# A context-attention stage: the outermost loop of TensorE's program written out for its fourteen middle chunks

## The reference, cut to what matters

```
q      = layernorm(x) @ Wq                  (32 tokens)
k, v   = split(ctx @ Wkv)                   (257 keys of 256 features)
k, v   = with null_kv as one more key and value
sim    = q . k / sqrt(64)                   (16 heads x 32 x 258)
out    = softmax(sim) @ v, heads joined
x      = x + layernorm(out @ Wout) * ln_scale + ln_bias
```

## Time and profile before

| what | value |
|---|---|
| median of three runs | 4516.92 us |
| the profiled execution's own time | 4519.83 us |
| its span (first to last instruction) | 4518.0 us |
| mean granted TensorE clock over the span | 0.917 of full speed |
| TensorE matmul busy | 3780.1 us, 84% of the span |
| VectorE, ScalarE, GpSimd busy | 63%, 44%, 18% of the span |
| the stage's score matmuls begin and end | 96.5 us to 1511.5 us |

### The profile page before, as it was taken

One profiled execution on the slowest core, in us unless ns is written; L12 is line 12 of the kernel. 1 busy time (PEld: TensorE's weight loads), 2 busy tenths in 40 slices (PEclk: granted clock), 3 DMA queues, 4 the chain that ended last, 5 costly groups with the idle time before them and its releaser, 6 DMA issues. The chain is left out here.

```text
span 4518.0 us, 116638 instructions
## 1 busy us (share of the span) xinstructions
PE 3780.1 (84%) x46470; PEld 2881.3 (64%) x46470; DVE 2838.7 (63%) x5431; ACT 1998.1 (44%) x4327; POOL 818.4 (18%) x797
## 2 busy tenths in 40 slices
PE   5999999999999873279998679889997777879776
PEld 4888888888888642257666356656664345656454
DVE  2766666666666587442223776567776956878683
ACT  2332333233223364533333333478887745654323
POOL 0000000000000041200000036555553012200160
PEclk7999999999999986689999889989998989989878
DMA  4655555555555145310000023222220000000000
GB/s 127 133 120 119 120 119 120 120 120 120 119 119 123 39 125 183 123 70 1 0 0 21 5 101 145 79 71 67 72 71 27 0 6 3 0 13 1 9 3 24
DMA packets 307757, 320.58 MB, mean 71 GB/s; under 512 B 43440, under 2 KB 295249, under 8 KB 299873
## 3 DMA queue, kind: packets, MB, share of 16 engines
q1 hardware_dynamic: 307296, 313.84, 27.3%
HBM read 286.44 MB, written 27.05 MB: 69 GB/s over the span
## 5 line engine op out<-in xcount | busy, mean ns | idle before, releaser
L3891 PE MATMUL c_psA<-c_kc,c_qt 128*128 128x257 f32 x2048 | 497.6, 398 | 78.0 <-issue 77.4
L3912 PEld LDWEIGHTS c_psB<-c_pt,c_vc 32*128 32x128 f32 x16384 | 471.8, 188 | 44.5 <-issue 44.5
L3912 PE MATMUL c_psB<-c_pt,c_vc 32*128 32x128 f32 x16384 | 496.2, 274 | 1.9 <-DVE c_vo L4091 1.9
L3891 PEld LDWEIGHTS c_psA<-c_kc,c_qt 128*128 128x128 f32 x2048 | 399.9, 201 | 139.5 <-issue 81.3
L4015 ACT ACTIVATE c_sc<-c_psA,c_mx 128x257 f32<-128x257 f32 x512 | 215.4, 473 | 534.4 <-DVE c_mx L4102 534.4
L637 PEld LDWEIGHTS f_psY<-f_w_down,f_hT 128*128 128x128 f32 x2560 | 302.7, 192 | 64.7 <-issue 48.4
L680 ACT ACTIVATE f_hT<-f_psH,f_b_up 128x512 f32<-128x512 f32 x320 | 214.3, 688 | 281.1 <-PE f_psH L627 276.5
L4098 DVE TENSOR_REDUCE c_nm<-c_psA 128x2 f32<-128x514 f32 x256 | 176.7, 690 | 255.8 <-PE c_psA L3891 255.8
L627 PE MATMUL f_psH<-f_xs,f_w_up 128*128 128x512 f32 x640 | 303.6, 610 | 17.3 <-ACT f_hT L680 17.3
L637 PE MATMUL f_psY<-f_w_down,f_hT 128*128 128x128 f32 x2560 | 306.9, 276 | 10.1 <-ACT f_hT L680 5.7
L2320 POOL TENSOR_TENSOR x_sc<-x_sc,x_rec 128x1156 f32<-128x1156 f32 x128 | 270.7, 2115 | 208.0 <-DVE x_rec L2586 208.0
(11 more groups left out here) (823 smaller groups left out, 7695.4 us busy)
## 6 DMA issues: line engine op xcount, KB each, us to landing
c_vc<-in_ctx SPq DMA_DIRECT2D x512, 256.0 KB
c_kc<-in_ctxT SPq DMA_DIRECT2D x128, 257.0 KB
g_wide<-g_w_dram SPq DMA_DIRECT2D x32, 1024.0 KB, 8.3
x_kc<-in_ctxT SPq DMA_DIRECT2D x32, 512.0 KB
x_vc<-in_ctx SPq DMA_DIRECT2D x64, 256.0 KB
l_k_dram<-l_dist SPq DMA_DIRECT2D x32, 256.0 KB, 4.3
l_q_dram<-l_turn SPq DMA_DIRECT2D x8, 1024.0 KB, 9.7
y_pt<-l_q_dram SPq DMA_DIRECT2D x8, 1024.0 KB, 5.9
```

The source lines that it names most:

```text
L3891: mm = pe.matmul(psA[:, r, 0:KEYS], qt[:, b // BT, half * BT + b % BT, r * G:(r + 1) * G].rearrange("p h i -> p (h i)"), kc[:, b // 2 % 2, ...
L3912: mm = pe.matmul(psB[:, e, half * P:(half + 1) * P], vc[e * S:(e + 1) * S, b % 4, t, half * P:(half + 1) * P], pt[e * S:(e + 1) * S, :, t] ...
```

## The change

TensorE's hardware loop over chunks 1 to 14 becomes a Python loop: the same fourteen chunks are emitted one behind the other as straight code, with constants where the loop index stood. The order of the work, its waits and their counts are the same. The programs of the four other engines keep their loops.

```
                 pe.wait_ge(fixed, 9 * 16)
                 pe.wait_ge(values_loaded, 48)
                 chunk(0, True, False)
-                with pe.Fori(1, NI - 1) as i:
+                for i in range(1, NI - 1):
                     chunk(i, False, False)
                 chunk(NI - 1, False, True)
                 context(B - 1, NB - 1, NG, B - BT, FILLS - FIRST + 1, None)
```

## The result

The changed kernel took 4439.42 us in the median of four runs (4427.49 to 4444.64), the kernel before 4515.79 us (four runs, 4514.62 to 4517.19). The ratio is 0.9827 with a 95% interval of 0.9807 to 0.9847: 76 us faster. The forecast was 4435.5 us with a range of 4431 to 4446. The profiled execution took 4439.48 us with a span of 4437.7 us.

The account below looks back on a forecast made before the run. TensorE was taken to bound the stage; 51.4 us of pauses plus 30.0 us of slow first batches, 81.4 us, taken from the 4516.9 us median gave 4435.5 us, range 4431 to 4446, chance 0.87.

Parts of the forecast that it names:

- TensorE is the bound and its 13 pauses lie on the path: Before the first scores of a chunk TensorE idles at 13 taken loop branches, 51.4 us in all, wholly on the path.
- The sum of 81.4 us: Gain over the loop of 14 chunks: 1259.68 us less 1178.2 us undisturbed, from 51.4 us pauses and 30.0 us slow batches.
- rival B: Straight code comes in too slowly in the `context` block, 5.6 us instead of 3.85; about 4635 us; chance 0.03.
- The cause, a taken branch whose start is fetched again: TensorE's loop branch, 4690 ns in the median, waits to fetch a target no longer held; 13 such branches go.
- The slow first batches, 30.0 us: After each pause the clock is lower for a few us; first score matmuls take 5.39 us, not 3.64; 30.0 us.
- Register instructions, other engines' branches, transfers: nothing each: Register instructions ahead of TensorE's waits, the other four engines' branches and the closer-spaced transfers were each priced at nothing.
- Rival A: Another wait, such as VectorE's, fills the pause at 13 chunk boundaries; 4485 us, smaller form 4448 to 4461; chance 0.08.
- Rival C: Pause belongs to the place, not the branch, or unbroken work lowers the clock; no change, 4515.8 us; chance 0.02.
- All that follows keeps its lengths: A sign of being right: everything behind the stage's last chunk takes as long as before.

Follow-up runs that it names:

- the run with the nops: Changed kernel with 120 nops on TensorE ahead of the first scores of chunks 2 to 14, absent from the program that ran; 4441.28 us.
- the round that is held: Kernel before with its loops, `context` multiplying only 3 of 8 key groups, 1771 TensorE instructions a round; taken branches 0.21 to 0.23 us but for the first.
- one of 2027: Kernel before with its loops, `context` multiplying only 4 of 8 key groups, 2027 TensorE instructions a round; taken branches 5.5 to 7.3 us.
- the pauses without a branch: Changed kernel with TensorE waiting at starts of chunks 2 to 14 for 8 or 4 needless ScalarE copies; 4536.15 us and 4495.00 us.

## Why the prediction was right, point by point

*TensorE is the bound and its 13 pauses lie on the path.* Right. The stage shortened by what the pauses and their slow batches held, and no other wait came.

*The sum of 81.4 us.* Its own part measured 1259.68 - 1179.47 = 80.2 us. The 1.2 us between are small delays of a few batches in straight code, which I had priced at nothing (3.0 us in the run with the nops). Fourteen plain chunks would be 1178.2 us. The timeline shows the largest delay in the `context` block of the first batch of chunk 11, which otherwise takes 3.85 us:

```profile
1016.78 4.24 PE L3912 MATMUL c_psB<-c_pt,c_vc 32*128 32x128 f32 x128
```

The same batch is late by the same 0.38 us (12.41 for 12.03 us between score starts) in both other executions of the changed kernel and in the kernel with all engines written out. It sits in the densest block, as rival B placed it; that a fetch makes it is argued, not shown. All such delays together are 1.2 us in 1179, where B needed 0.73 us in each of 112 batches to decide.

*The cause, a taken branch whose start is fetched again.* The count of branches moved the time as forecast (13, 6, 1, 0), and the length of the round switches the cost on and off. The instruction queue agrees: over the fourteen chunks it moved 194, 178, 168 and 164 packets with 13, 6, 1 and 0 taken branches, so 2 to 4 packets go with each, and the round that is held moved 16. I had expected about as many packets as before; that was wrong. That the extra packets are code fetched ahead and thrown away at the jump is likely, not shown. The Trainium skill (Runtime: NRT & Kernel Launch, Instruction fetch mechanics) speaks of 128 KiB or 2048 instructions for TensorE, in blocks of 256. The runs agree in kind: a round of 1771 instructions is held and one of 2027, close under that figure, is not. The same section of the Trainium skill also lets only a window of two blocks escape the stall. That doesn't fit TensorE here, since 1771 instructions would be about seven such blocks. The about 108 ns for a compare-and-branch that the Trainium skill gives (Advanced Engine Details and Errata, Control Flow Timing) fit neither kind of taken branch on TensorE: 0.21 us held, 3.6 to 7.3 us not held.

*The slow first batches, 30.0 us.* Right in size and cause. TensorE was busy for 1208.24 us of the loop before, which is 30.0 us over fourteen plain chunks, and 28.8 us over the straight code. The cause is shown by the pauses without a branch and the clock behind them. In both executions of the kernel before all 13 pauses had a slow batch; that isn't a rule, since of the six with two chunks a round two had none.

*Register instructions, other engines' branches, transfers: nothing each.* Right. VectorE began its first maximum of chunk 3 at 341.67 us, directly behind its last copy (341.31 + 0.39), as at the loop's exit before, and without the loops of the others the stage changed by 0.5 us, within the scatter. Rival A didn't come.

*Rival C.* It is excluded: chunk boundaries without a branch had no pause, and the clock stayed at 1.00 through 1179 us of unbroken matmuls.

*All that follows keeps its lengths.* Not so in the execution profiled: 5.0 us more behind the last chunk, and 5.1 us less ahead of chunk 1. That the two cancelled, so that the profiled time fell by 80.35 us, is luck. The median of the runs fell by 76.4 us here, and by 82.7 us where both kernels ran again beside each other (4519.09 to 4436.36). The measured 4439.42 is 3.9 us above the forecast. I had set the lower end of the range by the 2.6 us scatter of the kernel before and the 2.9 us between its profile and its median; the changed kernel's four runs lie 17 us apart, and one of them (4427.49) is below the range. So the mechanism was right, and that the median came so close is in part luck.

## What to carry to other kernels

Read a hardware loop's own line in the trace: a taken branch of 0.2 us costs next to nothing; if the branches take microseconds round after round, and not just the first, the round is too long to be held. On TensorE count the pause and the slow batches behind it (here 4.0 + 2.2 us), take the loop's length less its rounds at the undisturbed pace as the gain, and check that nothing else would hold those moments; here writing the loop out took 80.2 us, and seven chunks in a round took 71.5 of them. Loops on the engines that had slack here, or one whose round is held, are not worth writing out: the first changed nothing that could be measured, and the second would give back 0.2 us a round.

## What the runs showed of the hardware that was not expected

- The step is sharp: a round of 1771 TensorE instructions jumps back in 0.21 us, one of 2027 in 5.5 to 7.3 us, which is more than the 3.6 to 5.7 us of the round of 3051.
- The round that is held moved 16 packets of instructions in fourteen chunks, and none in the last 908 us; the one of 2027 moved 138.
- The first taken branch of the round that is held later still took 7.2 us, and nine packets came in the round behind it.
- Even pauses of 2.64 us were followed by score matmuls of 5.39 us instead of 3.64, in 12 of 13 cases; behind pauses of 4.72 us they took 5.40 to 6.74 us, in all 13. Two branch pauses of 2.97 and 3.30 us were followed by 3.71 us at full clock.
- 120 nops in the source of TensorE's program left no trace in the program that ran.
